# A mixture-of-experts layer: second product with its weights standing, eight tile sizes, and one paired gather

## The reference

```
x_rot  = hamilton(normalize(cond), hamilton(x * gate, conj(normalize(q_right))))
top1   = argmax(x_rot @ router_w + router_b)              # one expert in 0..7 for each token
for e in range(8):
    a, g = split(x_rot @ w1[e] + b1[e], 2)                # w1[e]: 256 x 2048
    y    = (a * sigmoid(g)) @ w2[e] + b2[e]               # w2[e]: 1024 x 256
    out += where(top1 == e, y, 0)
return x + out
```

## Time and profile before

| | |
|---|---|
| three runs | 214.12, 214.83, 215.44 us, median 214.83 |
| span of the profiled execution, from its first to its last instruction | 213.9 us |
| the median above this span | 0.9 us |
| PE, PEld | 202.7, 191.0 us busy |
| DVE, POOL, ACT | 158.0, 129.2, 122.5 us busy |
| mean granted TensorE clock | 0.987 |
| start of the first product of the first tile | 36.27 us |
| end of the last matmul | 209.6 us |

### The profile page before, as it was taken

One profiled execution on the slowest core, in us unless ns is written; L12 is line 12 of the kernel. 1 busy time (PEld: TensorE's weight loads), 2 busy tenths in 40 slices (PEclk: granted clock), 3 DMA queues, 4 the chain that ended last, 5 costly groups with the idle time before them and its releaser, 6 DMA issues.

```text
span 213.9 us, 4367 instructions
## 1 busy us (share of the span) xinstructions
PE 202.7 (95%) x1512; PEld 191.0 (89%) x1513; DVE 158.0 (74%) x308; ACT 122.5 (57%) x206; POOL 129.2 (60%) x163
## 2 busy tenths in 40 slices
PE   7997779999999999999998999999999999999991
PEld 3877625999999999999998999899999999999991
DVE  4918936789928996598888969993998479874950
ACT  2454861576727482667585767564949185735620
POOL 6002467876802888287878877885487817820751
PEclk9999969999999999999999999999999999999998
DMA  5993744889775174937499479738535691820011
GB/s 144 393 365 122 291 142 116 265 300 311 215 193 227 63 259 97 361 90 264 103 296 317 131 219 320 259 76 292 223 135 168 204 287 69 256 44 0 25 40 37
DMA packets 17540, 41.26 MB, mean 193 GB/s; under 512 B 2920, under 2 KB 11241, under 8 KB 15338
## 3 DMA queue, kind: packets, MB, share of 16 engines
q1 hardware_dynamic: 12784, 30.48, 39.9%
q0 software_dynamic: 4512, 10.50, 19.4%
q10 hardware_dynamic: 218, 0.01, 0.1%
HBM read 36.78 MB, written 6.03 MB: 200 GB/s over the span
## 4 chain that ended last, share of the span: by engine, by line
PE 57%; POOL 13%; DVE 12%; issue 7%; DMA 7%; ACT 2%; DVEq 0%; POOLq 0%; ACTq 0%
PE y_ps L1121 7%; DMA xg<-x_rows,g_idx 7%; PE y_ps L1122 6%; PE y_ps L1123 6%; POOL y_out L429 5%; PE g_ps L1101 5%; POOL out_dram L438 5%; PE g_ps L1106 5%; PE g_ps L1102 4%; PE a_ps L1106 4%; PE a_ps L1102 4%; PE a_ps L1101 4%; PE y_ps L931 3%; POOL xg L417 3%; DVE arena L821 3%
## 5 line engine op out<-in xcount | busy, mean ns | idle before, releaser
L438 POOL DMA_INDIRECT out_dram<-y_out,s_idx x30 | 42.1, 1403 | 41.5 <-DVE y_out L850 30.8
L573 ACT ACTIVATE arena<-g_ps,b_t 128x384 f32<-128x384 f32 (+1 forms) x64 | 34.5, 538 | 47.4 <-PE g_ps L1106 47.4
L821 DVE SCALAR_TENSOR_TENSOR arena<-a_ps,b_t,arena 128x384 f32<-128x384 f32 (+1 forms) x64 | 36.1, 564 | 30.5 <-PE a_ps L1106 27.6
L1121 PE MATMUL y_ps<-w_hi,u_hi 128*128 128x256 f32 x168 | 48.6, 289 | 0.1
L429 POOL DMA_INDIRECT y_out<-in_x_dram,g_idx x32 | 42.4, 1325 | 9.8 <-issue 9.8
L1122 PE MATMUL y_ps<-w_lo,u_hi 128*128 128x256 f32 x168 | 47.5, 283 | 0.0
L1123 PE MATMUL y_ps<-w_hi,u_lo 128*128 128x256 f32 x168 | 47.5, 283 | 0.0
L417 POOL DMA_INDIRECT xg<-x_rows,g_idx x32 | 37.2, 1164 | 13.7 <-issue 9.1
L712 DVE TENSOR_TENSOR w_lo<-w_raw,w_hi 128x1024 fp32r<-128x1024 f32 x32 | 37.2, 1220 | 4.8 <-DMA xg<-x_rows,g_idx 3.6
L579 ACT ACTIVATE u_hi<-arena 128x384 fp32r<-128x384 f32 (+1 forms) x64 | 30.7, 479 | 15.5 <-DVE arena L821 15.5
L1101 PE MATMUL g_ps<-xr_hi,w_hi 128*128 128x256 f32 (+3 forms) x128 | 36.9, 301 | 0.3 <-issue 0.2
(11 more groups left out here) (167 smaller groups left out, 297.0 us busy)
## 6 DMA issues: line engine op xcount, KB each, us to landing
w_raw<-in_L_ffn_w_dram SPq DMA_DIRECT2D x16, 1024.0 KB, 8.5
w_raw<-in_L_ffn_w_dram SPq DMA_DIRECT2D x16, 512.0 KB, 5.0
arena<-in_x_dram SPq DMA_DIRECT2D x4, 512.0 KB, 5.9
x_rows<-arena SPq DMA_DIRECT2D x8, 256.0 KB, 2.6
b_all<-in_L_ffn_b_dram SPq DMA_DIRECT2D x1, 1024.0 KB, 5.1
xg<-x_rows,g_idx POOLq DMA_INDIRECT x32, 6.1
y_out<-in_x_dram,g_idx POOLq DMA_INDIRECT x32, 4.2
out_dram<-y_out,s_idx POOLq DMA_INDIRECT x30, 4.0
```

The costliest lines, as they stand in the source:

```text
L438: nc.gpsimd.indirect_dma_start(out=out_flat, out_offset=bass.IndirectOffsetOnAxis(ap=s_idx[:, i * NSUB + s:i * NSUB + s + 1], axis=0), in_ ...
L573: nc.scalar.activation(sig[:, c % SIG_RING, 0:n], pair[c % RING][1][:, 0:n], ACT.Sigmoid, bias=b1_t[:, bass.ds(e * (2 * NC) + (NC + c), 1) ...
L821: V.scalar_tensor_tensor(u32[:, c % (8 - SIG_RING), 0:n], pair[c % RING][0][:, 0:n], b1_t[:, bass.ds(e * (2 * NC) + c, 1)], sig[:, c % SIG ...
L1121: T.matmul(dst, u_hi[:, uv], w2_hi[:, wv], start=first, stop=False)
```

## The change

The first product gets eight sizes with steps of 16 tokens, and the second product is now made by size as well, with 128 columns of `w2` standing and the tokens streaming. Its result has the output features on the partitions. ACT copies it out of PSUM with `b2` added (`biased`), and PE turns it back: six transposes of 128 columns in the middle of the next tile's first product (at c = 2), and for the last tile eight transposes behind its second product. The table `x_rows` has rows of 512 floats, the rotated row and the row of `x` side by side; one gather of four DMAs takes both, into three buffers used in turn. The rows of `x` are written to the table by four more DMAs in front of the rotated ones, and `w2` of the first expert is loaded behind them all. ACT and DVE take 256, 336 or 512 columns. The counts above now fall on the sizes 320, 336, 224, 224, 272, 272, 336 and 224; before they fell on 320, 352, 256, 256, 288, 288, 352 and 256. The core of the diff:

```diff
-    SIZES = (256, 288, 320, 352, 384, 512)
+    SIZES = (224, 256, 272, 288, 304, 320, 336, 512)
+    WIDTH = {blocks: max(size for size, b in zip(SIZES, BLOCKS) if b == blocks) for blocks in BLOCKS}
+    TURNED = 3
-    LANDINGS = (0, 1, 2, 3, 5)
+    LANDINGS = tuple(range(len(SIZES)))
-    x_rows = nc.dram_tensor("x_rows", (TOK, DIM), F32, kind="Internal").ap()
+    x_rows = nc.dram_tensor("x_rows", (TOK, 2 * DIM), F32, kind="Internal").ap()
...
-            load_w2(0, 0)
+            for g in range(4):
+                sp.wait_ge(x_loaded[g], 16)
+                sp.dma_start(x_rows_v[:, 4 * g:4 * g + 4, DIM:ROW], x_tok[:, 4 * g:4 * g + 4, :]).then_inc(x_part_written, 16)
             for b in range(NB // 2):
                 sp.wait_ge(x_rot_done, b + 1)
-                sp.dma_start(x_rows_v[:, 2 * b:2 * b + 2, :], x_rot[:, 2 * b:2 * b + 2, :]).then_inc(x_rows_written, 16)
-            load_w2(0, 1)
...
+                sp.dma_start(x_rows_v[:, 2 * b:2 * b + 2, 0:DIM], x_rot[:, 2 * b:2 * b + 2, :]).then_inc(x_rows_written, 16)
+            for h in range(W2U):
+                load_w2(0, h)
...
             for i in range(NE):
+                wait_gathered(i)
                 if i + 1 < NE:
-                    pool.wait_ge(xg_turned, (i + 1) * KH)
-                    wait_gathered(i)
+                    if i + 1 >= YB:
+                        wait_scattered(i + 1 - YB)
                     gather(i + 1)
...
+            def biased(i, e, h, first, cols, done=None):
+                act.wait_ge(half_done[h], i + 1)
+                put = nc.scalar.activation(yt[:, h * ITEM + first:h * ITEM + cols], y_half[h][:, first:cols], ACT.Identity,
+                                           bias=b2_t[:, bass.ds(e * KH + h, 1)])
...
                     for u in range(W1U):
                         w1_hi_part(i, u)
+                        if u % 2 == 1:
+                            biased(i - 1, i - 1, u // 2, 0, FIRST, yt_done[u // 2])
...
+                if f == 6:
+                    visit(7)
...
+                if b == 3:
+                    visit(8)
...
+                if b == 6:
+                    visit(9)
...
                 for c in range(NC):
+                    if c == 2:
+                        with pe.If(((i - 1) & 15) < NE - 1):
+                            turn_back_rows(at1, TURNED)
...
+            def second_product(size, at1):
+                n = SIZES[size]
                 pe.wait_ge(w2_split, at1)
+                pe.wait_ge(y_done, at1)
+                for h in range(KH):
+                    dst = y_half[h][:, 0:n]
+                    for c in range(NC):
+                        if h == 0:
+                            pe.wait_ge(u_lo_done[c], at1)
+                        wv = slice(c * DIM + h * P, c * DIM + (h + 1) * P)
+                        uv = slice(c * ITEM, c * ITEM + n)
+                        T.matmul(dst, w2_hi[:, wv], u_hi[:, uv], start=(c == 0), stop=False)
+                        T.matmul(dst, w2_lo[:, wv], u_hi[:, uv], start=False, stop=False)
+                        last = T.matmul(dst, w2_hi[:, wv], u_lo[:, uv], start=False, stop=(c == NC - 1))
+                    last.then_inc(half_done[h], 1)
...
+                    with pe.If(pe.snap(size_before, min_val=0, max_val=len(SIZES) - 1) >= BLOCKS.index(NSUB)):
+                        turn_back_rest(at1)
-                    by_size(word, 0, len(SIZES) - 1, lambda size: first_product(size, at1))
+                    by_size(word, 0, len(SIZES) - 1, lambda size: first_and_landing(size, i, at1))
...
-                        turn_held(after, next16)
-                    second_product(word, at1)
+                        buffer = pe.snap((i + 1) - 3 * (((i + 1) * 11) >> 5), min_val=0, max_val=YB - 1)
+                        with pe.If(buffer < 1):
+                            turn_held(after, next16, 0)
+                        with pe.Else():
+                            with pe.If(buffer < 2):
+                                turn_held(after, next16, 1)
+                            with pe.Else():
+                                turn_held(after, next16, 2)
+                    by_size(word, 0, len(SIZES) - 1, lambda size: second_product(size, at1))
+                    with pe.If(i >= NE - 1):
+                        turn_back_rows(next1, NSUB)
```

More of the change, by code:

```diff
@@ L422, in wait_gathered @@
             def wait_gathered(i):
-                for s in range(2, NSUB):
+                for s in range(NSUB):
                     pool.wait_ge(gathered[s], (i + 1) * 16)
[L426 to L432, removed]
+            pool.wait_ge(x_part_written, 4 * 16)
             pool.wait_ge(x_rows_written, NB // 2 * 16)
@@ L853, in add_last, with rows_of @@
-            def add_last(i, blocks):
[L855 to L859, removed]
-                dve.wait_ge(mm2_done, i + 1)
-                for a in range(2 if blocks == NSUB else 1):
-                    rows = bank_rows(i, 0)[:, a]
-                    V.tensor_tensor(rows, y_ps[0][:, a * DIM:(a + 1) * DIM], rows, ALU.add).then_inc(last_added, 1)
-                dve.wait_ge(last_added, 3 if blocks == NSUB else 2)
-                for h in range(2):
-                    dve.sem_inc(y_done[h], 1)
+            def rows_of(i, first, count):
+                return (pairs[buffer_of(i)].rearrange("p (s k h d) -> p s k h d", s=NSUB, k=2, h=KH)[:, first:first + count, 1],
+                        y_ps[:, :].rearrange("p (h s d) -> p s h d", h=KH, s=NSUB)[:, first:first + count])
@@ new lines, in add_rows @@
+            def add_rows(i):
+                for s in range(NSUB):
+                    dve.wait_ge(gathered[s], (i + 1) * 16)
+                dve.wait_ge(y_turned, i + 1)
+                rows, y = rows_of(i, 0, NSUB)
+                V.tensor_tensor(rows, y, rows, ALU.add).then_inc(y_done, 1)
+            def add_last(i, blocks):
+                for s in range(blocks):
+                    dve.wait_ge(gathered[s], (i + 1) * 16)
+                dve.wait_ge(y_turned, i + 1)
+                for s in range(blocks):
+                    rows, y = rows_of(i, s, 1)
+                    V.tensor_tensor(rows[:, 0], y[:, 0], rows[:, 0], ALU.add).then_inc(last_added, 1)
+                dve.wait_ge(last_added, blocks)
+                dve.sem_inc(y_done, 1)
@@ L868, in gate_tile @@
             def gate_tile(i, e, blocks):
-                n = blocks * P
+                n = WIDTH[blocks]
                 split_x(i, n)
@@ L1050, in _, with turn @@
             keep_warm_long(late_ps, 2)
-            def turn(subs, i16, end=True):
+            def turn(subs, i16, end=True, buffer=0):
                 for s in subs:
@@ L1150, in by_size, with first_and_landing @@
                     by_size(word, middle, high, body)
+            def first_and_landing(size, i, at1):
+                first_product(size, i, at1)
+                if size in LANDINGS:
+                    landing(LANDINGS.index(size) + 2)
+            pe.wait_ge(yt_set, 1)
+            size_before = pe.alloc_register("size_before")
+            pe.reg_mov(size_before, 0)
             with pe.Fori(0, TAB) as i:
```

179 lines of the change are left out of this document (81 added, 98 removed).

## The result

| | before | after |
|---|---|---|
| median | 214.8 us (214.12 to 215.44) | 435.2 us (433.2 to 436.6) |
| ratio, 95% interval | | 2.022 (2.011 to 2.034) |
| span of the profiled execution | 213.9 us | 434.7 us |
| PE busy | 202.7 us | 240.4 us |
| mean granted TensorE clock | 0.987 | 0.740 |

A forecast was written before the change was run, and what follows sets the result against it. PE was taken to set the time from 36.27 us on. 213.9 - 6.7 - 0.6 + 4.6 + 3.2 + 2.5 + 2.2 = 219.1 us of span, and 0.9 more for the median: 220.0 us, range 206 to 233.

The forecast's parts named there:

- Code never visited: First tile's jump to second-product code not yet fetched: one stall of 2.27 us less little, +2.2 us (0 to 9).
- the start: Before the first product: wider table +0.3, longer gathered rows +0.7, a visit's stall +1.5; together +2.5 us.
- second rival: Loop code thrown out: some ten stalls of 2.27 us where the size changes, 230 to 242, say 235 us; chance 0.22.
- The forecast's own sum: Whole kernel: all terms added to the 213.9 us span before give a span of 219.1 us.
- Price by columns: Each PE matmul priced by columns streamed: 109 ns for 224 (107 to 121.7), 127.7 for 272, 155 for 336.
- third rival: Matmuls of 224 columns take as long as 256: +5.5 us on any other case; no separate chance given.
- Second products: 48 matmuls of the tile's columns each: 5.23 us at 224, 6.13 at 272, 7.45 at 336; 50.0 us in all.
- The two ways: PE idle behind branches, turn to second product and second to next first product: 9.0 and 7.4 us in all.
- first rival: Added branches stay hidden under queued matmuls, the ways cost 4.5 us as now, no code stalls: 204.4 us; chance 0.20.
- The tail: Behind the last product: copy, eight transposes, two adds and both scatters take 7.5 us against 4.3, +3.2 us.

The follow-up runs named there:

- v4: The changed kernel with four sizes (224, 272, 336, 512) in place of eight and without the early visits to the sizes' code; 225.1 us, ratio 1.041.
- dead: The kernel before with 600 TensorE instructions that never run laid in its tile loop; 314.8 us.
- b8: The kernel before with only the change's eight sizes and the landings and nine visits that go with them; 292.9 us.
- r8: The changed kernel with each size's turn and second product laid right behind its first product, so a tile chooses its size once; 332.8 us.
- dead40: The kernel before with 80 TensorE instructions (40 matmuls) that never run laid in its tile loop; 250.8 us.
- dead100: The kernel before with 200 TensorE instructions (100 matmuls) that never run laid in its tile loop; 260.1 us.
- b4: The kernel before with only its list of sizes changed, to four (224, 272, 336, 512); 212.1 us, ratio 0.989.

## Why the prediction was wrong

**The step that failed** is that the new code stays loaded. The sum has one term for code, "Code never visited", +2.2 us for one stall (and 1.5 us in the start for a visit); measured were 192.6 us of stalls more than in v4. The second rival had the cause right, and its chance, its count and its price were too small. In parts:

- *How many stalls.* "Where the size changes, some ten." There were 49. Eight came in visits, 41 in the tile loop, about five a tile, also where the size repeats: between 161.4 and 252.4 us, two tiles of 224, there are ten of them, 41.7 us. I had thought of a tile's own code as the thing thrown out. It is nearly every far branch: past the landing, over the turn, each level of both choices, the end, the head.
- *What one costs.* I took 2.27 us, the only row there was the earlier trace rows, and down to half of that where queued matmuls cover. It was 4.07 us. Little is covered: against v4, which does the same work in code that fits, the stalls are 192.6 us more and PE's idle time 170.1 us more (434.7 - 240.4 less 221.4 - 197.2). 
- *What it does to the clock.* I had no term. PE's busy time is 43.2 us higher than v4's (240.4 against 197.2) for the same matmuls but for 336 columns in place of 320 in v4's first tile, at a mean clock of 0.740 against 0.968. Idle and busy time together, 170.1 + 43.2 = 213.3 us, are by their definition the difference between the two spans; the trace shows how it is shared out.
- *Its chance.* 0.22. The earlier trace rows show that the code of before stays, seven fetches for a program of eight blocks, and not how much more would. With the new code at 1.6 times that, a loop counted up from 1350 to 2300 instructions in rival 2 itself, and a trace in which one far branch had stalled, nothing in the working spoke for its fitting.

A rule of thumb comes out of the table: a microsecond of stall costs about 1.0 to 1.1 us of time. It is 99.2 us of span for 88.9 of stalls in dead, 77.3 for 72.7 in b8, 109.7 for 106.7 in r8 over v4 and 35.1 for 35.9 in dead40, but 44.6 for 35.0 in dead100.

**The forecast's own sum** was made for code that stays loaded. v4 is nearly that kernel, with 336 columns for the first tile in place of 320, fewer levels of size, and no visits. It has a span of 221.4 us where the sum said 219.1. Stretches of v4, turn to second product, a second product, and second to first product, all of 224 columns; then second products of 272 and 336, and the tail:

```profile
104.08:105.35 1.27, 0.62 (x5) 0.45 (x5) 1.23 (x4) 1.00 (x4) 0.96 (x2) 1.00 0.67 73
105.35:110.94 5.59, 5.59 (x49) 5.41 (x48) 4.56 (x6) 5.02 (x8) 0.56 (x2) 1.00 0.54 189
110.94:111.80 0.86, 0.01 (x2) 0.04 (x1) 0.86 (x2) 0.54 (x1) 0.86 (x1) 1.00 0.00 0
145.77:152.03 6.26, 6.26 (x51) 6.04 (x49) 5.55 (x8) 5.54 (x8) 2.28 (x2) 1.00 0.39 120
189.75:197.36 7.61, 7.61 (x51) 7.32 (x49) 6.46 (x9) 5.31 (x8) 0.00 (x0) 1.00 0.27 93
214.41:221.40 6.99, 1.06 (x8) 0.85 (x8) 0.76 (x2) 0.54 (x1) 1.97 (x2) 0.73 0.09 30
```

- *Price by columns.* 272 and 336 right, 224 a little low. From b4, whose first products are not broken by the turning back (224, 272, 336):

```profile
84.41:95.28 10.87, 10.87 (x98) 10.69 (x96) 7.60 (x14) 6.60 (x14) 7.39 (x7) 1.00 0.80 260
...
121.11:133.38 12.27, 12.27 (x97) 12.05 (x96) 10.19 (x16) 7.72 (x14) 10.13 (x8) 1.00 0.78 240
...
166.27:181.24 14.97, 14.97 (x99) 14.96 (x99) 10.54 (x17) 9.25 (x16) 9.05 (x7) 1.00 0.63 195
```

  Over 96: 113.2, 127.8 and 155.9 ns, where I took 109, 127.7 and 155. (The prediction's bounds for 224, 107 and 121.7, hold it.) The third rival (224 as slow as 256, 121.7) is false, and the 95.8 that the Trainium skill's gap gives (TensorE: Matmul & The Clock Gate, Back-to-back issue gap) is not reached either. Second products: 5.59, 6.26, 7.61 against 5.23, 6.13, 7.45.
- *The two ways* were over-priced: 1.27 and 0.86 us at a tile of 224 columns where I took 2.0 and 1.5. So less of the branches shows than I had, which leans to the first rival; v4 has two levels of size where the change has three.
- *The tail*: 6.99 us against 7.5 forecast. In b4 it is 4.17.
- *The start*: the first product at 38.42 against 36.27, 2.15 us later where I had 2.5, but the reason is another: 2.55 us of it is the stall at the levels, not the table.
- *Code never visited*: the stall came, 4.18 us where I had 2.2, and the second product behind it ran at a clock of 0.72, 10.18 us in place of the 7.61 above. +6.7 in all.

So apart from the code the change brings no gain either. With the same four sizes and no stall behind 68 us, v4 needs 152.9 us from the end of the first tile's second product to the end, b4 151.1. Tiles of 272 gain, tiles of 224 and the tail lose. One tile of 224 and one of 272, from the start of its first product to that of the next tile's (the first stretch begins 0.1 us early), in v4 and then in b4:

```profile
92.38:111.80 19.42, 17.81 (x155) 17.33 (x155) 14.33 (x25) 13.65 (x26) 8.27 (x7) 1.00 0.67 221
...
131.38:152.78 21.40, 19.91 (x157) 19.51 (x157) 16.71 (x25) 14.76 (x25) 11.53 (x9) 1.00 0.60 210
```

```profile
84.41:102.34 17.93, 17.37 (x150) 16.95 (x149) 13.89 (x25) 12.51 (x23) 12.93 (x12) 1.00 0.76 243
...
121.11:143.71 22.60, 22.00 (x175) 21.47 (x175) 19.73 (x28) 14.40 (x23) 18.33 (x15) 1.00 0.66 202
```

A tile of 224 takes 1.4 us more and one of 272 1.2 us less. PE is busy only 0.4 us longer at 224; the other microsecond is the idle time of the two ways.

## What to carry to other kernels

Count the instructions of every loop that an engine runs, those it branches over too, before pricing anything in it. Here tile loops of TensorE up to 6.0 blocks of 256 instructions ran as if branches were free, and with 0.3 more one lost 17%. The two places where the profile tells this at once are the code queue's fetches after the loop's first round and branch times of microseconds in the sequencer's rows; an idle engine "waiting for issue" is the sign to look there. When more variants are wanted than fit, lay what one pass needs side by side, and choose the variant once.

## What I had not expected of the hardware

- A branch into code that isn't loaded took 4.07 us on average in the changed kernel, and up to 8.4 us in b8, where the only one before had taken 2.27.
- Two tiles whose code lies up to eight blocks apart ran without a fetch, so what is kept is not one window.
- Code that is jumped over costs as code that runs: 80 instructions in the loop 36 us, 600 behind it nothing.
- The clock after a stall: idle stretches of 12.7 and 18.8 us at a mean of 0.54 and 0.55, and 43 us more of PE's busy time over the kernel than in v4.
